# Attention and ternary feed-forward on one core: third pieces of the second heads turned by DMA, a new order of work, and the latents' turns placed between products

## The reference

```python
q_lat, kv_lat = x @ Wq_down, x @ Wkv_down             # 256 and 128 wide
q = [q_lat @ Wq_up, rope(q_lat @ Wq_rope)]            # 16 heads, 64 + 64 wide
k = [kv_lat @ Wk_up, rope(x @ Wk_rope)]
v = kv_lat @ Wv_up                                    # 16 heads, 128 wide
attn = softmax(causal(q @ k.T * 128 ** -0.5))
out = (attn @ v) @ Wo                                 # all heads, back to 512
# ffn: every weight is replaced by sign(round(W / mean|W|), clipped to -1..1) * mean|W|
hidden = silu(x @ up.T) * (x @ gate.T)                # 2048 wide
y = hidden @ down.T
```

## Time and profile before

| | us |
|---|---|
| median of 3 runs | 1750.13 |
| the profiled execution | 1747.9 |
| its span in the trace | 1746.1 |
| TensorE busy | 1662.5 (95%) |
| VectorE busy | 1158.5 (66%) |
| ScalarE busy | 1070.2 (61%) |
| GpSimd busy | 920.5 (53%) |

### The profile page before, as it was taken

How to read it: one execution, slowest core, us unless ns; L and a number is a source line. 1 busy time by engine, 2 the same in 40 slices (tenths; PEclk the granted TensorE clock), 3 DMA queues, 4 the chain that set the end, 5 groups by cost and what they waited for, 6 DMA issues and landing times.

```text
span 1746.1 us, 30275 instructions
## 1 busy us (share of the span) xinstructions
PE 1662.5 (95%) x9474; PEld 1337.0 (77%) x9474; DVE 1158.5 (66%) x2719; ACT 1070.2 (61%) x2543; POOL 920.5 (53%) x731
## 2 busy tenths in 40 slices
PE   6899998899999998999999999999999999999998
PEld 5688786677777776777877877877877788888887
DVE  6466866676787776787787877777878733333332
ACT  3233335788798786788787787887877532323222
POOL 2466565455456469788787788788776400000000
PEclk9999998999999999999999999999999999999999
DMA  3399998898779766769858777767766830000000
GB/s 130 111 225 230 227 247 217 201 199 170 160 161 173 141 139 145 162 133 178 158 127 172 147 146 163 157 141 164 153 122 143 220 145 21 4 7 19 1 25 24
DMA packets 466809, 244.79 MB, mean 140 GB/s; under 512 B 382688, under 2 KB 416608, under 8 KB 466400
## 3 DMA queue, kind: packets, MB, share of 16 engines
q1 hardware_dynamic: 455136, 221.94, 57.6%
q10 hardware_dynamic: 11520, 20.98, 4.5%
HBM read 97.06 MB, written 54.53 MB: 87 GB/s over the span
## 4 chain that ended last, share of the span: by engine, by line
PE 59%; POOL 7%; ACT 6%; issue 3%; DVE 3%; DMA 3%; SPq 2%; ACTq 0%; POOLq 0%; DVEq 0%
PE ps_scores L1657 15%; PE ps_o L1719 14%; PE ps_scores L1881 13%; PE ps_scores L1737 7%; PE ps_scores L1697 4%; PE ps_scores L1896 3%; PE ps_o L1896 3%; ACT probs L1465 3%; POOL halved L1226 2%; POOL below L1422 1%; POOL signs L1426 1%; DMA signs<-in_W_up 1%; ACT halved L1475 1%; POOL k_lo L1367 1%; POOL signs L1430 1%
## 5 line engine op out<-in xcount | busy, mean ns | idle before, releaser
L1226 POOL TENSOR_TENSOR halved<-probs,halved 128x512 f16<-128x512 f32 (+3 forms) x416 | 406.9, 995 | 209.6 <-ACT halved L1475 192.7
L1465 ACT ACTIVATE probs<-ps_scores,bias 128x512 f32<-128x512 f32 (+3 forms) x640 | 399.1, 626 | 124.2 <-DVE bias L1568 92.6
L1719 PE MATMUL ps_o<-moved,kv_hi 128*128 128x256 f16 x2176 | 335.1, 275 | 15.8 <-DVE o_lo L1611 9.6
L1558 DVE TENSOR_REDUCE negmax<-ps_scores 128x1 f32<-128x512 f32 (+1 forms) x384 | 253.1, 674 | 53.3 <-PE ps_scores L1657 52.8
L1657 PE MATMUL ps_scores<-k_hi,q_hi 128*128 128x512 f32 (+2 forms) x576 | 244.4, 424 | 25.8 <-ACT probs L1465 22.8
L1719 PEld LDWEIGHTS ps_o<-moved,kv_hi 128*128 128x128 f16 x2176 | 185.6, 98 | 107.6 <-issue 75.8
L1475 ACT CAST halved<-probs 128x512 f16<-128x512 f32 (+3 forms) x416 | 224.3, 546 | 10.6 <-ACT plain_out L517 0.7
L1657 PE MATMUL ps_scores<-k_hi,q_lo 128*128 128x512 f32 (+2 forms) x576 | 213.4, 371 | 0.0
L1719 PE MATMUL ps_o<-moved,kv_lo 128*128 128x256 f16 x1088 | 213.1, 273 | 0.0
L1657 PE MATMUL ps_scores<-k_lo,q_hi 128*128 128x512 f32 (+2 forms) x576 | 212.9, 370 | 0.0
L1627 DVE SCALAR_TENSOR_TENSOR y<-ps_scores,share,y 128x512 f32<-128x512 f32 x256 | 191.7, 749 | 28.1 <-PE ps_scores L1737 23.4
(11 more groups left out here) (165 smaller groups left out, 3572.8 us busy)
## 6 DMA issues: line engine op xcount, KB each, us to landing
plainT<-plain_out ACTq DMA_DIRECT2D x64, 256.0 KB, 4.5
rotT<-rot_out SPq DMA_DIRECT2D x64, 256.0 KB, 4.6
all_signs<-signs SPq DMA_DIRECT2D x24, 512.0 KB, 3.2
q_raw<-plainT SPq DMA_DIRECT2D x128, 64.0 KB, 2.4
q_raw<-rotT SPq DMA_DIRECT2D x256, 32.0 KB, 2.1
signs<-in_W_up SPq DMA_DIRECT2D x16, 512.0 KB, 4.1
signs<-in_W_gate SPq DMA_DIRECT2D x16, 512.0 KB, 4.1
signs<-in_W_down SPq DMA_DIRECT2D x16, 512.0 KB, 4.2
```

The costliest lines, as they stand in the source:

```text
L1226: nc.gpsimd.tensor_tensor(halved_of(args, pair, 1), by_block(probs_of(args, pair)), halved_of(args, pair, 0), ALU.subtract).then_inc(halve ...
L1465: nc.scalar.activation(probs_of(args, pair), ps_scores[:, pieces.number[args] % RING, 0:keys], ACT.Exp, scale=-1.0 if last_piece(*args) el ...
L1558: nc.vector.tensor_reduce(to, scores, AX_X, ALU.max, negate=True).then_inc(max_done, 1)
L1719: last = nc.tensor.matmul(ps_o[:, i, 0:2 * P], kv[x][:, b, :], there, start=(s == 0 and (m, b) == (0, blocks[0])), stop=(s + 1 == nsteps(t ...
```

## The change

Four edits.

- `by_dma` sends piece 2 of head 1 of the large tiles of slots 0 to 3 (tiles 15 to 12) by DMA too.
- `Plan.TIMES` has new numbers for all eight slots. In slots 0 to 3 there are seven instead of six entries for `halved_hi`, `halved_lo` and `move`, and three instead of four for `turn`, `turned_hi` and `turned_lo`. In all slots the order of events changes.
- `latents`: `steps(c)` is the new order of a chunk for TensorE, ScalarE and VectorE alike: product 0, turns 0 and 1, product 1, turns 2 and 3, product 2. The statistics of the next chunk and its root now come ahead of the work on product 2.
- `heads_inputs`: ScalarE does one exponential of a 128x1 column into a scratch tensor at the stage's start.

```diff
@@ latents @@
+    LAT, TURN = "lat", "turn"
+    def steps(c):
+        order = ((LAT, 0), (TURN, 0), (TURN, 1), (LAT, 1), (TURN, 2), (TURN, 3), (LAT, 2))
+        return [(kind, i) for kind, i in order if (1 <= c <= NC if kind == LAT else c < NC)]
...
@@ latents, block.vector @@
             for c in range(NC + 1):
-                for i in range(TC):
-                    if c + AHEAD < NC:
-                        tile_stats(TC * (c + AHEAD) + i)
-                    if 1 <= c <= NC and i < NL:
+                if c == 0:
+                    for i in range(TC):
+                        tile_stats(TC * AHEAD + i)
+                for kind, i in steps(c):
+                    if 1 <= c < NC - AHEAD and (kind, i) in ((LAT, 0), (TURN, 1), (LAT, 1), (TURN, 3)):
+                        tile_stats(TC * (c + AHEAD) + ((LAT, 0), (TURN, 1), (LAT, 1), (TURN, 3)).index((kind, i)))
+                    if c + AHEAD < NC and c and (kind, i) == (LAT, 2):
+                        chunk_stats(c + AHEAD)
+                    if kind == LAT:
...
-                    if 1 <= c < NC:
+                    if c and kind == TURN:
                         turned_low(TC * c + i)
-                if c + AHEAD < NC:
-                    chunk_stats(c + AHEAD)
                 if c == 0:
+                    chunk_stats(AHEAD)
...
@@ latents, block.scalar @@
-                for i in range(TC):
-                    if 1 <= c <= NC and i < NL:
+                for kind, i in steps(c):
+                    if kind == LAT and i == 2 and c + AHEAD < NC:
+                        root(c + AHEAD)
+                    if kind == LAT:
...
-                if c + AHEAD < NC:
-                    root(c + AHEAD)
+                if c == 0:
+                    root(AHEAD)
@@ latents, block.tensor @@
             for c in range(NC + 1):
-                for i in range(TC):
-                    if 1 <= c <= NC and i < NL:
+                for kind, i in steps(c):
+                    if kind == LAT:
                         latent(c - 1, i)
-                    if c < NC:
+                    else:
                         turn(TC * c + i)
@@ heads_inputs @@
+    first_exp = sb("first_exp", [P, 1])
...
         act.wait_ge(unit_ready, 1)
         act.wait_ge(inverse_ready, 2)
+        nc.scalar.activation(first_exp[:], unit, ACT.Exp)
@@ by_dma @@
-    return h == 0 or i == 1
+    return h == 0 or i == 1 or (n < 4 and p == 2)
@@ class Plan, TIMES of slot 0 @@
-            "scores": (-11.57, -11.2, -10.56, -9.56, -7.72, -6.99, -6.25, -5.22, -2.99, -2.81),
-            "maximum": (-10.81, -10.45, -10, -9.01, -7.16, -6.43, -5.68, -4.39, -2.62, -1.98),
-            "exp": (-8.3, -7.51, -6.73, -5.94, -3.68, -3.32, -2.48, -1.88, -1.14, -0.74),
-            "halved_hi": (-7.84, -7.05, -6.27, -5.32, -0.91, -0.51),
-            "halved_lo": (-7.42, -6.63, -5.84, -4.89, -0.65, -0.25),
-            "move": (-6.56, -5.64, -4.72, -3.81, -0.28, 0.2),
-            "turn": (-3.22, -1.88, -0.23, 1.57),
-            "turned_hi": (-2.8, -1.46, 0.19, 1.99),
-            "turned_lo": (-2.34, -0.87, 1.11, 2.72),
-            "values": (0, 0.37, 0.74, 2.17, 3.27, 4.65, 5.02, 5.39, 5.76),
-            "o_hi": (7.14, 7.33),
-            "o_lo": (7.42, 10.39),
-            "out": (9.79, 11.43, 13.22, 14.7),
-            "add": (10.6, 11.99, 13.91, 15.66),
+            "scores": (-11.41, -10.69, -10.18, -8.74, -6.42, -6.02, -5, -4.71, -2.98, -1.97),
+            "maximum": (-10.67, -10.29, -9.74, -8.01, -6.13, -5.39, -4.5, -4.08, -3, -2.13),
+            "exp": (-7.24, -6.54, -5.77, -5.11, -3.95, -3.86, -3.58, -1.32, -1, -0.93),
+            "halved_hi": (-5.54, -5.52, -4.92, -4.87, -1.62, -0.81, -0.27),
+            "halved_lo": (-7.36, -6.33, -6.22, -6.11, -2.81, -2.1, -1.13),
+            "move": (-3.6, -3, -2.99, -2.62, 0.35, 1.46, 1.47),
+            "turn": (-3.24, -1.21, 1.14),
+            "turned_hi": (-3.04, -0.3, 1.52),
+            "turned_lo": (-2.24, 0.31, 2.81),
+            "values": (0.53, 1.01, 1.35, 3.09, 4.31, 5.19, 5.78, 6.6, 6.81),
+            "o_hi": (7.13, 7.14),
+            "o_lo": (8.05, 8.52),
+            "out": (9.53, 11.46, 12.28, 14.58),
+            "add": (10.01, 11.54, 13.17, 15.01),
...
```

198 lines of the change are left out of this document (99 added, 99 removed).

## The result

Before 1749.17 us, after 1737.22 us (medians of 19 runs each, side by side): faster by 11.9 us. The ratio is 0.9938, 95% interval 0.9927 to 0.9949. Forecast were 27.2 us. So the direction was right, the time lies inside the range, and less than half of the gain arrived.

The account below looks back on a forecast made before the run. TensorE, busy for 95% of the span, was taken to bound the kernel. Terms -14.1 - 0.5 - 5 - 6.5 - 1.1 = -27.2 us gave 1720.7 for the profiled execution and a median of 1723, range 1700 to 1750.

Parts of the forecast that it names:

- part 1: Attention, slots 0 to 3: 32 pieces of four transposes leave TensorE at 0.44 us each, 14.1 us saved.
- Below 1 in any case, so I take nothing: DMA engines in attention: share rises from 0.76 to at most 0.85, costed at nothing.
- rival B: Attention: moves land late, 27 us in all, so no change and the kernel stays at 1750; chance 0.11.
- if TensorE waits for moves by more than 10 us: Sign that the forecast is wrong; TensorE's waits for a DMA in attention were 2.2 us before.
- The turns and the order: Attention: 14.1 us for pieces leaving TensorE, 0.5 for fewer waits on the turning bank, 5 for the new order.
- one pair's accident: Pair 2 lasts 142.5 us against 132.4 through a bad start of the signs; nothing added for its kind.
- The latents: Latents stage: new order removes waits and slow-clock stretches until GpSimd is late; 6.5 us saved, bounds 3 and 10.
- isn't touched and can only be shifted: Feed-forward, 362.0 us: taken as unaffected by the change, with no term of its own.
- The early exponential: Start of the heads' inputs: ScalarE's table load is hidden there, 1.1 us saved, bounds 0 and 1.3.
- C: Attention, pairs 3 to 7: GpSimd holds up ScalarE's exponentials, +50 us, 1773 in all; chance 0.12.
- D: Attention: the DMA queue binds and stretches it by 106 us, 1829 in all; chance 0.02.
- A: Attention: the order wins much more, half of TensorE's 46.9 us of idleness instead of 5, 1705 in all; chance 0.21.

Follow-up runs that it names:

- plan alone: Kernel before with by_dma and all new tuples of the plan, without the new latents and the early exponential: 1747.83 us, ratio 0.9998.
- the second timing: The changed kernel run again with no edit, for a second trace: 1740.55 us, ratio 0.9953 to the kernel before.

## Why the prediction was right in sign and wrong in size

**The step that failed** stands in part 1: "SP: four more issues of 1.26 us, 5.0 us a pair ... behind each of them on SP stand loads and the next moves. I cost all this at nothing on the path, because each engine stays under 85% and TensorE over 95%." The reason given is a count of busy time, and SP was left out of it. In the kernel before SP's rows, which stand one directly behind the other, fill 129.6 of the 144.3 us of pair 0, 111.5 of 135.6 in pair 1 and 117.0 of 132.4 in pair 5: 90, 82 and 88% (a row can hold a wait: a move's is 1.17 us at the least and 4.29 at the most). In pairs 0 and 1 the loads for the sums pass through one buffer, so their cycle (`abs` done, issue, landing, `abs`) has to fit between two sums. In the kernel before it nearly fitted (4.3 us of waits, 1.75 us to spare in the median). The added moves and the new order pushed the issues back, and it no longer did (18.7 us, 0.02 us to spare). Without the loads the change is worth 22.4 us, with them 11.9: at least 10.5 us of the shortfall of 15.3 (27.2 - 11.9) are shown to come with these loads. The prediction read late pairs for its terms and dismissed the early ones: I had windows of pairs 1, 2 and 5, saw the 117.20 us of ScalarE in pair 1 against 106.6 in pair 5, and did not ask which instructions these were and what fed them.

How the 10.5 us divide between SP's list and the DMA engines is not shown. With all loads on SP five traces of the new plan have 135.0 to 140.4 us in pair 1; with the sums' loads on ScalarE's queue two have 133.3 and 133.4, and without these loads it is 129.3. Pair 0 has 147.3 to 152.4, then 152.1 and 147.5, then 139.5 us. So SP's list is a part of the loss in pair 1, and in pair 0 relieving it brought nothing, since the DMA engines took over. For them too the prediction said "Below 1 in any case, so I take nothing", from the share of all of attention, 0.76; pair 0 had 0.87 before the change.

**Moves late: rival B was a part of it.** I would be wrong "if TensorE waits for moves by more than 10 us". It waits 16.6 us in attention against 2.2, 8.0 us of it in 295:600. The rival gave this two reasons, the distance from `move` to `values`, 2.96 steps at the least, and SP's list. For the longest wait it is the second with a slow landing (5.7 us): 3.96 steps were planned, and ten loads on SP used them up. It costs less than the waits add up to: without the sums' loads 8.9 us of these waits are still there in 295:600, and attention gains all that was forecast.

**The turns and the order: sum right, terms wrong.** A late pair went from 132.4 to 130.1 us (forecast 129 to 131); 14.1 + 0.5 + 5 over eight pairs is 2.45 us a pair, and 2.3 came. But 0.44 us a piece for "what TensorE no longer does" is no term of its own: in the old order the same 32 pieces cost some 11 us instead of saving 14, and 1.1 us in a late pair. The windows of pair 5 show the mechanism in part: TensorE was busy for 128.99 of 132.40 us and is for 127.92 of 130.10, so 1.1 us of the 2.3 are work that left (four pieces at 0.44 would be 1.8) and 1.2 are idle time that closed. Which waits closed I did not trace. One reading of the plan was one-sided: from `exp` to the `scores` four pieces on the median distance grows from 0.65 to 1.02 steps, but the smallest falls from 0.23 to -0.09.

**Pair 2** gained 4.4 to 7.5 us in the five traces that have the new plan with the sums and their loads as they were (5.7 in plan alone), for which I had added nothing ("one pair's accident"). It came in plan alone too (136.8), so it belongs to the new order. ScalarE's waits for GpSimd there fell from 11.3 us to 6.3.

**The latents were sized right** (5.8 us in the trace, 6.4 on average; 6.5 forecast), with the mechanism as described: GpSimd starts a chunk 11.8 us after the one before, 11.5 forecast. Not all of an early start is seen at once in the next stage: ten traces with the new latents start the first scores at 279.5 us on average (276.5 to 284.0), four with the old ones at 283.4 (282.5 to 284.4), so 3.9 us of 6.4. But their first values products come at 300.8 us on average (297.8 to 303.8) against 306.3 (305.6 to 306.7): 5.6 us arrive where attention becomes bound by TensorE. In the second half of the heads' inputs (194:282) the DMA engines' share is 1.01 before and 1.02 after. A stage that is held by its stores and loads there would take up part of an early start of TensorE. That fits, but no run here tried it.

**The tail** (+5.6 us, of which moving three numbers gives back 2.3 to 4.0) was not in the prediction at all. That the feed-forward "isn't touched and can only be shifted" overlooked that its first events are merged with the last pair's by numbers of their own. An edit of a plan moves every event against every list merged with it.

**The early exponential** was sized at 1.1 us; its load did move to 66.15, ahead of the heads' inputs, and no gain can be measured. For the load itself, the row below shows 1.28 us and the exponential directly behind it:

```profile
66.15 1.28 ACT L571 ACT_TABLE_LOAD   x1 [4.05 <-DVE kv_scale L687]
67.44 0.20 ACT L571 ACTIVATE first_exp<-kv_scale 128x1 f32<-128x1 f32 x1
```

So the drain that the Trainium skill ("ScalarE: Activation LUTs", "What ACT_TABLE_LOAD costs") adds is not to be seen here either, and the 2.7 us by that page did not appear. Here ScalarE was idle ahead of the load; in the kernel before it was busy up to the load at 289.24 and had the exponential directly behind it, so a drain had no room on either side.

**Rivals C, D and A.** GpSimd held up ScalarE no more than before: it reached 108.66 us in pair 5 (109 forecast), and ScalarE's waits for it there are 4.0 us against 3.7, under the 6 us that I had set. In all of attention they are 24.8 us against 28.9. But GpSimd's share of the chain rose from 7 to 12%, and its low halves alone from 2 to 5%; what that costs no run here tells. The DMA engines did not bind in attention on average: their share there is 0.82, and without the sums' loads (0.80) attention gained what was forecast. In pair 0 (0.89) they are near it, as the run with the loads on ScalarE's queue shows. The order alone did not win 18 us more.

**How it adds up.** To the forecast -27.2 come +10.5 for the sums' loads, about +5 for the tail, about +2 for the latents and the exponential (7.6 forecast, 5.6 at the first values product), and about -4 for pair 2 beyond a late pair's gain: -13.7, with -11.9 and, in the second timing, -7.6 measured. These corrections come from different runs, each uncertain by about 3 us, so that they come out near it is partly luck. Three things stay open: how the loads' cost in pair 0 divides between SP's list and the DMA engines, which waits the new order closed in the late pairs, and why the latents and the plan together give more than apart.

## What to carry to other kernels

Count the queue that issues the DMAs like an engine, in each stage and not in the mean, and ask of each single buffer whether its cycle still fits: a move of 1.26 us on SP cost most where a load stood behind it and ScalarE behind the load. Do not price moved work and its new order as two terms; either alone can lose where both together gain. A load taken off a full list can still meet full DMA engines: read their share in that stage before counting on it. Before calling a stage untouched, look for a second list whose fixed numbers are merged with the one edited.

## What was unexpected in the hardware

- A transposing DMA is listed at its issuer with 1.26 us in the median (4.96 at most, waits included), two to three times the 0.43 to 0.58 us of a plain load of 512 KB in the same list:

```profile
L1323 SPq DMA_TRANSPOSE moved<-halved x448: 1167/1261/4959, 298.3 to 1365.2; - x150
...
L1348 SPq DMA_DIRECT2D signs<-in_W_up x8: 358/431/1398, 325.1 to 408.0; - x8
```

- With the chunks' loads on ScalarE's queue beside the moves on SP's, one load took 12.1 us to land and one move 13.0 us, in a stretch of 134 GB/s; the medians over 300:590 are 4.2 to 4.6 us for these loads and 3.9 us for the moves.

- A gap of 3.91 us on TensorE cost more than itself: the clock was lower behind it, and four transposes took 1.09 instead of 0.44 us. With the gap of 1.97 us at the feed-forward's start the same was seen, matmuls at 0.63 for 0.39 us. In pairs 0 and 1 together, 34 records fewer left TensorE's busy time nearly unchanged, 262.53 against 263.01 us.
